# Last batch's router chain ahead of its shared expert, sixteen filler matmuls, earlier query/key projections, and final-norm statistics two blocks ahead

## What is computed

```python
x = x + layernorm(attention(layernorm(x)))
x = x + layernorm(moe(layernorm(x)))

# attention, per batch and head (16 heads of 16 channels)
z_k, z_q = one scalar per token and head, from k and q      # "z" units, through a fused weight
ctx[i] = sum_j max(0, 1 - |z_q[i] - z_k[j]| / bandwidth) * v[j]

# moe, per token
gu = x @ shared_gate_up_w                                    # 256 -> 2*512
shared = (silu(gate) * up) @ shared_down_w * sigmoid(x @ shared_gate_w)
probs = softmax(x @ gate_w); top 8 of 64 experts             # logits, 64 + 1 columns
pos = running count of each expert's hits over all tokens    # capacity 128 rows per expert
y = sum over the 8 experts of w * (silu(.) * . @ down)
out = y + shared
```

## Time and profile before

| | |
|---|---|
| median of 3 runs | 2308.65 us (2304.75 to 2308.7) |
| profiled execution, its own time | 2307.02 us |
| span of its profile | 2305.6 us |
| PE / DVE / ACT / POOL busy | 1995.1 / 1949.6 / 1932.7 / 976.5 us |
| mean granted TensorE clock | 0.951 |

### The profile page before, as it was taken

How to read it: one execution, slowest core, us unless ns; L and a number is a source line. 1 busy time by engine, 2 the same in 40 slices (tenths; PEclk the granted TensorE clock), 3 DMA queues, 4 the chain that set the end, 5 groups by cost and what they waited for, 6 DMA issues and landing times.

```text
span 2305.6 us, 30639 instructions
## 1 busy us (share of the span) xinstructions
PE 1995.1 (87%) x11794; PEld 728.3 (32%) x11794; DVE 1949.6 (85%) x2792; ACT 1932.7 (84%) x1284; POOL 976.5 (42%) x412
## 2 busy tenths in 40 slices
PE   6799889899779899986798999868999996899966
PEld 4333233233112222221122222212222223577732
DVE  4597997897999898999998999999989997644427
ACT  3697997998999999999999999999999996122214
POOL 1100100100317458453185395422773674377745
PEclk9899999999889999999999999989989997899988
DMA  6425244435120202131202021312120305599987
GB/s 234 158 92 184 93 155 137 148 121 197 60 110 12 98 29 85 42 122 55 92 21 96 21 97 37 122 57 83 33 85 21 106 3 137 161 248 231 215 241 259
DMA packets 182231, 259.27 MB, mean 112 GB/s; under 512 B 22472, under 2 KB 162376, under 8 KB 173896
## 3 DMA queue, kind: packets, MB, share of 16 engines
q1 hardware_dynamic: 167600, 237.83, 30.9%
q0 software_dynamic: 12288, 18.88, 4.4%
q10 hardware_dynamic: 2200, 0.60, 0.1%
HBM read 187.25 MB, written 70.03 MB: 112 GB/s over the span
## 4 chain that ended last, share of the span: by engine, by line
PE 31%; DVE 24%; ACT 19%; POOL 13%; DMA 6%; issue 6%; SPq 0%; DVEq 0%; POOLq 0%; ACTq 0%
ACT TB L1105 18%; PE ps L902 14%; DVE TB L1429 12%; POOL scr L1610 8%; PE ps L812 6%; PE ps L849 5%; DVE TB L1451 3%; DMA y_rows<-ZB 3%; DVE st L1161 2%; PE ps L857 2%; POOL y_rows L1718 1%; PE ps L833 1%; PE ps L796 1%; DVE TB L1427 1%; DMA TB<-h_rows,ZB 1%
## 5 line engine op out<-in xcount | busy, mean ns | idle before, releaser
L1105 ACT ACTIVATE TB<-ZB,nzk 128x2048 f32<-128x2048 f32 x932 | 1778.4, 2011 | 79.2 <-DMA ZB<-zq_rows 57.2
L902 PE MATMUL ps<-TB,V 128*32 128x512 f32 x8192 | 1099.1, 630 | 208.9 <-DVE TB L1429 197.5
L1429 DVE TENSOR_SCALAR TB<-TB 128x2048 f32<-128x2048 f32 x932 | 1109.1, 1220 | 26.2 <-ACT TB L1105 25.0
L1610 POOL TENSOR_TENSOR scr<-ebase,scr 128x256 f32<-128x256 f32 x12 | 518.7, 43226 | 0.0
L902 PEld LDWEIGHTS ps<-TB,V 128*32 128x32 f32 x8192 | 186.5, 111 | 869.5 <-DVE TB L1429 571.3
L849 PE MATMUL ps<-XF,wsgu 128*128 128x512 f32 x512 | 278.8, 638 | 0.0
L1580 POOL TENSOR_SCALAR ve<-mv 128x4 f32<-128x4 f32 x44 | 40.4, 918 | 515.7 <-DVE mv L1165 515.6
L1451 DVE SCALAR_TENSOR_TENSOR TB<-ZB,kz 128x2048 f32<-128x2048 f32 x92 | 217.2, 2361 | 6.6 <-PE ps L902 6.6
L1608 POOL TENSOR_TENSOR scr<-ebase,scr 128x4 f32<-128x4 f32 x12 | 50.2, 4185 | 345.0 <-DVE scr L1295 345.0
L1134 ACT ACTIVATE ZB<-ps 128x128 f32<-128x128 f32 x64 | 17.7, 277 | 169.8 <-PE ps L983 169.8
L1597 POOL TENSOR_SCALAR ve<-mv 128x4 f32<-128x4 f32 x12 | 24.3, 2022 | 272.5 <-DVE mv L1165 272.5
(11 more groups left out here) (194 smaller groups left out, 1707.5 us busy)
## 6 DMA issues: line engine op xcount, KB each, us to landing
ZB<-zq_rows SPq DMA_DIRECT2D x64, 1024.0 KB, 7.0
scr<-fused_w SPq DMA_DIRECT2D x48, 512.0 KB, 3.3
TB<-y_rows SPq DMA_DIRECT2D x24, 512.0 KB, 7.9
TB<-in_egu_w SPq DMA_DIRECT2D x44, 256.0 KB, 3.6
y_rows<-zero SPq DMA_DIRECT2D x20, 512.0 KB, 4.9
fused_w<-TB SPq DMA_DIRECT2D x4, 2048.0 KB, 13.7
XF<-in_x SPq DMA_DIRECT2D x24, 256.0 KB, 5.4
v_rows<-scr SPq DMA_DIRECT2D x24, 256.0 KB, 2.2
```

Source lines behind the costliest of these rows:

```text
L902: ins = pe.matmul(ps[k][32 * c:32 * c + 32, :], V[:, o:o + 32], tile(n)[:, 512 * c:512 * c + 512], start=(kb == 0), stop=(kb == KB - 1))
L1105: act.activation(tile(e), zrow(head), ACT.Abs, bias=nzk[b][:, kb * H + g:kb * H + g + 1], scale=1.0).then_inc(s_abs, 1)
L1429: dve.tensor_scalar(T, T, 1.0, 1.0, ALU.min, ALU.subtract).then_inc(s_bump, 1)
L1610: pool.tensor_tensor(E4[:, :, 0:64], view(ebase[:, 0:1], 0, [[0, 4], [0, 64]]), E4[:, :, 0:64], ALU.pow).then_inc(s_ex, 1)
```

## The change

It has five edits.

- `z_at`: the pieces of z start four slots earlier and are laid out with nine slots for eight matmuls instead of eight; they end one slot earlier. What follows them (DVE "z", PE "zT", DVE "zT", SP "zq") is three slots later than before. Through the timetable the own set moves too: still 92 tiles, the 20 of batch 0 unchanged, those of the later batches up to 23 slots earlier.
- `tail_first`: transposes and logits of all four blocks come first; the up units stand between and behind the mask transposes, the gate units last. hT uses banks 4, 5 and 2, 3 in turn.
- `tensor_tail`: sixteen matmuls of 512 columns of `wsgu` against the identity, whose result nobody reads, ahead of that list.
- `scalar_tail`: the norm of block k + 1 stands ahead of the copy of hT of block k.
- The final norm: statistics two blocks ahead instead of one, and L1555 four blocks ahead instead of three.

```diff
 def z_at(f, tt):
-    return front_at(f, 3) + 21 + 2 * tt
+    return front_at(f, 3) + 17 + 9 * tt // 4
...
         r = z_at(f, 15)
-        dv += [(r + 5, "z", f), (r + 10, "zT", f)]
-        pe += [(r + 6, ("zT", f))]
-        sy += [(r + 11, "zq", f)]
+        dv += [(r + 9, "z", f), (r + 14, "zT", f)]
+        pe += [(r + 10, ("zT", f))]
+        sy += [(r + 15, "zq", f)]
...
     b = NB - 1
-    hT = [[(("hT", b, k, c), 4 + c) for c in range(2)] for k in range(4)]
...
-    o = hT[0] + [lg[0], up[0]] + hT[1] + [lg[1], up[1]] + hT[2] + [lg[2], mT[0]] + hT[3] + [lg[3], up[2], mT[1], up[3]]
-    return o + [mT[2], gate[0], mT[3]] + gate[1:4]
+    hT = [[(("hT", b, k, c), (4, 2)[k % 2] + c) for c in range(2)] for k in range(4)]
...
+    o = hT[0] + [lg[0]] + hT[1] + [lg[1]] + hT[2] + [lg[2], mT[0]] + hT[3] + [lg[3], up[0], mT[1], up[1], mT[2], up[2], mT[3]]
+    return o + gate[:3] + [up[3], gate[3]]
...
         def tensor_tail():
+
+            k, m = use["q", 15, 0]
+            pe.wait_ge(empty[k], m + 1)
+            for i in range(16):
+                pe.matmul(ps[k][:, :], ident[:, :], wsgu[:, 0, 0:512], start=True, stop=True)
             for unit, _ in tail_first():
                 tensor_stage(unit)
...
             scalar_stage("hT2", b, 0)
-            for k in range(1, 4):
-                scalar_stage("hn", b, k)
-                scalar_stage("hT2", b, k)
+            scalar_stage("hn", b, 1)
+            scalar_stage("hn", b, 2)
+            scalar_stage("hT2", b, 1)
+            scalar_stage("hn", b, 3)
+            scalar_stage("hT2", b, 2)
+            scalar_stage("hT2", b, 3)
...
-            vector_sums(0, v)
+            for n in range(2):
+                vector_sums(n, v)
             for n in range(NG):
-                if 12 <= n + 3 < NG:
+                if 12 <= n + 4 < NG:
...
-                if n + 1 < NG:
-                    vector_sums(n + 1, v)
+                if n + 2 < NG:
+                    vector_sums(n + 2, v)
```

More of the change, by code:

```diff
@@ L192, in tail_first @@
     b = NB - 1
-    hT = [[(("hT", b, k, c), 4 + c) for c in range(2)] for k in range(4)]
[L194 to L197, removed]
-    o = hT[0] + [lg[0], up[0]] + hT[1] + [lg[1], up[1]] + hT[2] + [lg[2], mT[0]] + hT[3] + [lg[3], up[2], mT[1], up[3]]
-    return o + [mT[2], gate[0], mT[3]] + gate[1:4]
+    hT = [[(("hT", b, k, c), (4, 2)[k % 2] + c) for c in range(2)] for k in range(4)]
+    lg = [(("lg", b, k), (6, 7, 0, 6)[k]) for k in range(4)]
+    mT = [(("mT", b, k), (1, 7, 0, 1)[k]) for k in range(4)]
+    gate = [(("gu", b, 0, m, 0), (6, 7, 0, 6)[m]) for m in range(4)]
+    up = [(("gu", b, 0, m, 1), (4, 5, 2, 3)[m]) for m in range(4)]
+    o = hT[0] + [lg[0]] + hT[1] + [lg[1]] + hT[2] + [lg[2], mT[0]] + hT[3] + [lg[3], up[0], mT[1], up[1], mT[2], up[2], mT[3]]
+    return o + gate[:3] + [up[3], gate[3]]
 def tail_middle():
@@ L1549, in vector_tail @@
                     vector_slots(g, i, v)
-            vector_sums(0, v)
+            for n in range(2):
+                vector_sums(n, v)
             for n in range(NG):
-                if 12 <= n + 3 < NG:
-                    dve.wait_ge(q_f[(n + 3) % NY], 32 * ((n + 3) // NY + 1))
-                    t = yt[(n + 3) % NY][0]
-                    dve.tensor_tensor(t, t, y_of(last, n - 9), ALU.add).then_inc(s_fs, 1)
-                if n + 1 < NG:
-                    vector_sums(n + 1, v)
+                if 12 <= n + 4 < NG:
+                    dve.wait_ge(q_f[(n + 4) % NY], 32 * ((n + 4) // NY + 1))
+                    t = yt[(n + 4) % NY][0]
+                    dve.tensor_tensor(t, t, y_of(last, n - 8), ALU.add).then_inc(s_fs, 1)
+                if n + 2 < NG:
+                    vector_sums(n + 2, v)
                 k, m = use["ys", n, 1]
```

## The result

| | before | changed |
|---|---|---|
| median, same chip | 2306.9 us (2303.5 to 2311.7, 10 runs) | 2313.7 us (2310.6 to 2319.7, 10 runs) |
| ratio | | 1.0036, 95% interval 1.0024 to 1.0047 |
| profiled execution | 2307.0 us, span 2305.6 | 2311.5 us, span 2310.0 |
| mean granted TensorE clock | 0.951 | 0.957 |

The account below looks back on a forecast made before the run. No engine was taken as the single bound: PE, DVE and ACT are each busy 84 to 87%, so each stretch has its own limit. -7.4 + 4.5 - 6.5 = -9.4 us gave 2299 us, range 2287 to 2306.

Parts of the forecast that it names:

- z stretches, by PE's idle time and clock: Batch 0: earlier z matmuls fill PE's waits for DVE and avoid cold steps; -7.4 us, bounds -12 to +1.
- own tiles moved: Later batches: the same number of own tiles, so taken as 0, within 2 us either way.
- last batch: Behind the last slot: clock falls, cold logits delay count 3 by 4.8 us; taken +4.5, bounds +6 and -6.3.
- final norm: Ring of DVE, POOL and ACT broken, rounds then follow PE at 3.44 us a block; -6.5 us, bounds -9, +2.5.
- the rivals: Whole kernel: clock stays warm, 2288.4 us (0.2); ends give nothing, 2309 (0.12); fillers run cold, 2311.8 (0.04).
- the one that ended slower: Last batch: sixteen fillers run at 1.2 GHz, first logits begin 12.5 us late; 2311.8 us, chance 0.04.
- another wait behind: Batch 1 of z: a further wait behind the quad's end, for which 2.6 - 0.8 = 1.8 us gain was taken.
- the clock falls around the pause: Last batch: PE idle from first hT's end (about 1936.8) to first logits (1939.95); clock falls between 1938 and 1941.
- cold logits take 3.65 us: Last batch: with the clock down each logits unit takes 3.65 us, against 1.97 us at 2.4 GHz.
- once down it stays down: Last batch: clock stays at 0.50 through logits and transposes until the up units; count 3 begins 1976.3, against 1971.58.
- kept 0.4 back: Final norm: a little of the 6.9 us gain withheld for the DMA engines' pause after load 7, giving -6.5.

Follow-up runs that it names:

- the mended kernel: The changed kernel with block 3's first store of values ahead of the fourth load on SP; three runs: -13.8, -11.0, -11.3 us against the kernel before.

## Why the prediction was wrong

| part | forecast | measured |
|---|---|---|
| z stretches, by PE's idle time and clock | -7.4 | -4.4 (stretches) |
| the store behind the fourth load | not seen | +15.3 (medians), +18.5 (stretches) |
| own tiles moved | 0, within 2 | +3.4 (medians), +3.5 (stretches) |
| last batch | +4.5 | -2.2 |
| final norm | -6.5 | -6.5 (medians), -7.6 (trace) |

**The step that failed** is in the part on the z stretches: the sentence on what the moved pieces are put past. It named DVE's z copy, PE's "zT", the copies of batch 3, and on SP only the query row's "zb". A piece's load is also an instruction of the same queue as the stores of values, and from the fourth on it holds a wait for PE. Moved from slot 50 to slot 46 it crossed the store at slot 47. The bounds of that term, -12 to +1, had no place for it, and neither had the rivals: the one that ended slower was about cold fillers. The timetable alone gives the crossing; that PE reaches its slot 46 only after DVE has reached its slot 48 gives the wait. DVE's wait of 1.85 us for that very store was in the trace of before, and the prediction does not mention it.

**Batch by batch**, with the store out of the way: batch 2 -6.1 us against -6.3 forecast, for the reason forecast (idle time filled, no cold steps). Batch 1 +0.1 against -1.8: ACT still waited 9.04 us for the query row, from 10.96, and what PE gained did not come through. The "another wait behind" that the prediction named is the likely reason; no run separates it. Batch 3 +1.0 against +0.7, and +0.6 between slots 176 and 208, for which nothing was forecast.

**The own tiles** were taken at 0 within 2 us, with no row under that; they likely cost 3.5, outside the stretches that the argument was about. By the two lists they move up to 12 slots earlier, not up to 23 as the description of the change has it.

**The last batch.** Two steps held: the clock falls around the pause in spite of the fillers, and cold logits take 3.65 us. The step that failed is "once down it stays down" until the first up unit. It rested on the stretch of 13.6 us at 0.50 in the earlier trace rows. The forecast needed the clock down from the first logits through the first up unit, 1939.95 to 1967.4, twice as long, and the stretch behind that row has the granted clock back at 1.00 with PE still busy without a gap:

```profile
1685.50:1700.00 14.50, 14.50 (x87) 3.48 (x86) 10.15 (x13) 14.11 (x10) 11.84 (x2) 1.00 0.73 273
```

In the changed kernel the clock was down for 17.1 us, with nothing but logits, transposes and waits of 0.89 us on PE. In ten of twelve executions with this list the clock was back before logits 3, so that logits 3 and up 0 ran in 1.97 and 1.94 us, and count 3 came at 52.2 to 53.0 us, not 57.6. One execution did as forecast:

```profile
1956.30 3.64 PE L833 MATMUL ps<-wg_sb,XF 128*128 128x65 f32 x16 [0.89 <-ACT XF L1048]
1959.74 3.72 PE L849 MATMUL ps<-XF,wsgu 128*128 128x512 f32 x4
```

with count 3 at 56.6 us. The prediction quoted from the Trainium skill (TensorE: Matmul & The Clock Gate, Part 4) that transposes do not count as busy in the same way. Here the clock came back under transposes and logits together; what each of them did, no run here separates, so this case neither bears that out nor contradicts it. The advice of the Trainium skill to keep the engine busy (the same page, Why this matters for your kernels) held here for the seven fillers in the pause; the sixteen ahead of it left the pause as it was and bought nothing.

**The norm** went as forecast: additions 3.43 us apart (3.44 forecast), no wait of PE at block 12, and -6.5 us by the medians (-7.6 in the trace, where the prediction's own sum came to -6.9 before it kept 0.4 back). From the last aggregation's start to the end of the last addition it took 2306.94 - 2299.39 = 7.55 us (7.2 forecast).

With the last batch and the own tiles as measured and z mended the parts give -4.4 + 3.5 - 2.2 - 6.5 = -9.6, against the -11.0 to -13.8 of the mended kernel, whose intervals hold it. With the store's 15.3 it is +5.7, and with the 18.5 of the stretches +8.9, on either side of the 6.8 measured. The parts fit to about 2 us, and cannot tell more.

## What to carry to other kernels

Where an instruction that holds a wait is moved in an in-order queue, list all that it crosses in that queue, and for each of these who waits for it: the DMA that costs nothing to issue can be the one that everything hangs on. Here it takes one line to see it, the timetable sorted for SP alone. Filler work kept TensorE's clock here only where it stood in the pause itself, 6.17 us of it (two executions); 13.90 us ahead of the pause did not, and 3.60 us in it kept the clock only until the next pause. What it wins has then to get past the next wait in the chain. A planner that works its choices out from the timetable (here the own tiles) is part of the change wherever the timetable is.

## What the runs showed beside that

- The same program does not get its clock back at the same place. With the list of the changed kernel the clock came back in ten executions between logits 2 and logits 3, in one only behind up 0, and in one directly behind the first logits. It fell in the pause in eight of them, 0.2 to 0.5 us behind it in three; in the one without fillers it had fallen long before. The early return:

```profile
1944.06 3.65 PE L833 MATMUL ps<-wg_sb,XF 128*128 128x65 f32 x16 [3.10 <-ACT XF L1048]
1947.50 1.91 PE L769 MATMUL ps<-ident,TB 128*128 128x128 f32 x8
1950.30 1.97 PE L833 MATMUL ps<-wg_sb,XF 128*128 128x65 f32 x16 [0.89 <-ACT XF L1048]
```

  There count 3 came at 47.7 us, 8.8 us sooner than in the slowest.
- What an issuer's order costs is not the time to issue. The store took SP 0.43 us and was held 6.8 us by the load ahead of it. The Trainium skill (DMA: Bandwidth & Descriptors, Issuing engines are not separate DMA queues) says that starting DMAs from several engines saves only the time that issuing takes. For the bytes that may be so; for this store, once in each of three batches, a place ahead of the waiting load was worth 15.3 us. No run here issued it from another engine.
- Executions of the same 1024 slots differ by up to 5.8 us (1832.1 to 1837.9 in seven with z and own tiles as before), and in five of the mended z edit with the new own tiles by 9.8 (1832.3 to 1842.1). A difference of two traces below that says little; the means over many of them, stretch by stretch, agreed with the medians within 1 us for the own tiles and 3 us for the store.
